# A perceiver layer on one core: the key tile between the two stages normalised by root and reciprocal, and the next projection put ahead of unit 0's transposes

## The chip, the core and the metric

The kernel runs on one core of a Trainium2 chip. A core has five engines with queues of their own, each of which works through its queue in order: PE (TensorE, matrix products and transposes), DVE (VectorE), ACT (ScalarE), POOL (GpSimd) and SP (which here only issues transfers). They wait for one another through semaphores. The metric is device time in microseconds (us), lower is better; of several runs the median is taken.

## What is computed

The layer is a cross-attention from 2 x 64 latent rows to 1024 context rows for each of two batches, then a self-attention and a gated feed-forward part. Only the first matters here:

```
k, v   = split((layernorm(ctx) ++ layernorm(latents)) @ Wkv)     # 1024 + 64 keys, 16 heads of 64
k      = k / max(norm(k per head) / 8, 1e-8) * kn_g
sim    = (q / max(norm(q per head) / 8, 1e-8) * qn_g / 8) @ k^T
attn   = softmax(sim, axis=-1)
out    = attn @ v, then @ Wout + bout, added to x
```

The two gain vectors go to the query side. The values are never formed: softmax(sim) is multiplied with the normalised context rows (`xn`), and the result with the value weights afterwards.

## The kernel before

**Items.** The rows of the context are cut into 16 tiles of 128, 8 for each batch, and one more tile holds the latents. With the queries that makes 18 items (`ITEMS`). For each item PE transposes the normalised rows (`norm_transposed`, 2 transposes into a PSUM bank), ACT and DVE split the result into a high and a low part (`xt_high` writes `xth`, `xt_low` writes `xtl`), and PE projects it on the keys (`project`, 12 matrix products of 512 columns, in `banks` 0 and 1 or 3 and 4). ACT squares the keys (`squares`), DVE sums the squares per head and clamps them (`key_norm2`, `key_clamp`), something takes the power -1/2 of the 128x16 sums, and DVE multiplies the keys by it out of PSUM (`key_scale`, two halves). PE transposes them (`keys_transposed`, 2 x 4), and ACT copies them out (`keys_out`).

**Stage one** is a loop over items 0 to 9 (`ITEMS_A` = 10), with the projection of item 10 behind it. Here the power is taken by a square root on ACT and a reciprocal on DVE.

**Stage two** is a loop over 16 units (`UNITS`; a unit is a pair of heads of one batch, 8 units for batch 0 and 8 for batch 1). In unit u PE transposes the exponentials (`probs_transposed`, parts 0, 1 and 2 with 4, 4 and 1 transposes), ACT and DVE split them (`probs_high` writes `pth`, `probs_low` writes `ptl`), PE computes the logits of unit u+1 (`logits`, parts 0, 1 and 2, with 3, 3 and 1 matrix products, in banks 3, 4 and 5) and then the mix of unit u (`mix`, 27 products). DVE takes the maximum with the mask (`logits_max`) and ACT the exponential (`exponentials`). From unit 1 on the logits of parts 0 and 1 use split operands: ACT writes `qh` and `kh` (`unit_high`), DVE `ql` and `kl` (`unit_low`), and only then can PE begin them. Units 0 to 7 carry one item each as well: unit u transposes the keys of item 10+u and projects item 11+u. For items from 10 on the power is taken by one POOL instruction (`ALU.pow`, line 451), and POOL's queue also holds the normalisation of the next context rows.

**The place between the stages.** PE transposes item 9's keys, computes unit 0's logits from unsplit operands, and then issues 12 matrix products on the identity matrix into bank 7 that compute nothing (`keep_clock(12, 7)`), while DVE and ACT make unit 0's exponentials. DVE works in the order `key_norm2(10)`, `key_clamp(10)`, `logits_max(0)`, `key_scale(10)`. ACT loads the table for the exponential, takes the exponentials, and goes into the unit loop, where its order for unit 0 is `probs_high(0, 0)`, `keys_out(10)`, `xt_high`, `unit_high(1)`, `probs_high(0, 1)`, `squares(11)`, `probs_high(0, 2)`.

The order is written out by hand in one function for each engine. Part 1 of unit 0's transposes goes to bank 7, parts 0 and 2 to bank 6. The profile counts a matrix product on fp32 data that are not split as two records, so `keep_clock(12, 7)` appears as 24.

Of the kernel before, what the change touches and what calls it, by code (L numbers as in the profile page):

```python
# [17 lines left out]
def perceiver_layer(nc, x, ctx, mask, ln_x_g, ln_x_b, ln_l_g, ln_l_b, qn_g, kn_g, Wq, Wkv, Wout, bout,  # L18
# [7 lines left out]
    G = H // 2  # L26
# [24 lines left out]
    with ExitStack() as stack:  # L51
# [257 lines left out]
        def t2_bank(i, h):  # L309
            return 2 if h == 0 else (6 if i < ITEMS_A else 0)  # L310

# [16 lines left out]
        def t3_bank(u, c):  # L328

            return 6 if c != 1 or 0 < u < G else (7 if u == 0 else 0)  # L330

# [71 lines left out]
        def _(pool):  # L403
# [44 lines left out]
            for i in range(ITEMS):  # L448
                if i >= ITEMS_A:
                    pool.wait_ge(n2_ready, i + 1)  # L450
                    nc.gpsimd.tensor_tensor(rn[:, i % 2, :], n2[:, i % 2, :], mhalf, ALU.pow).then_inc(rnp_ready, 1)  # L451
# [32 lines left out]
        def _(act):  # L484
# [141 lines left out]
            squares(ITEMS_A, 1)  # L626
            keys_out(ITEMS_A - 1, 0)
            keys_out(ITEMS_A - 1, 1)

            nc.scalar.activation(warm[:, 1:2], warm[:, 0:1], ACT.Exp)  # L630
            exponentials(0)
            context_high(ITEMS_A)
            for u in range(UNITS):
# [10 lines left out]
                if i < ITEMS:  # L644
                    keys_out(i, 0)
                    keys_out(i, 1)
                if i + 1 < ITEMS:
                    xt_high(tile(i + 1))
# [61 lines left out]
        def _(dve):  # L710
# [59 lines left out]
            def key_scale(i, h):  # L770
                if i >= ITEMS_A:
                    dve.wait_ge(rnp_ready, i - ITEMS_A + 1)
# [96 lines left out]
            key_clamp(ITEMS_A)  # L869
            logits_max(0)  # L870
            key_scale(ITEMS_A, 0)
            key_scale(ITEMS_A, 1)
            inverse_sum(0)
            for u in range(UNITS):
                i = ITEMS_A + u
                probs_low(u, 0)
                if i + 1 < ITEMS:
                    xt_low(tile(i + 1))
# [109 lines left out]
        def _(pe):  # L988
# [20 lines left out]
            def project(i, h):  # L1009

                if i >= ITEMS_A + 1:
# [28 lines left out]
            def keys_transposed(i, h):  # L1040
                pe.wait_ge(kn_ready, 2 * i + h + 1)
                if i > 0 and (h == 0 or i < ITEMS_A):
# [28 lines left out]
            def probs_transposed(u, c):  # L1071
                j0, j1 = T3[c]
                if c == 0:
                    pe.wait_ge(exp_ready, u + 1)
                if u == 0 or u > G:

                    if 3 * u + c - (1 if c == 2 else 2 if c == 1 else 0) > 0 and not (u == 0 and c == 1):
                        pe.wait_ge(ptl_ready, 3 * u + c - (1 if c == 2 else 2 if c == 1 else 0))
                elif u < G or c != 1:
                    pe.wait_ge(ptl_ready, 3 * u + c - (1 if u == G and c == 2 else 0))  # L1080
# [3 lines left out]
            def mix(u, parts=(0, 1, 2)):  # L1084
                b = u // G
                if u % G == 0:
                    pe.wait_ge(xnl_ready, NT * (b + 1))
                    pe.wait_ge(lns_ready, 1)
                if u == 0:
                    pe.wait_ge(ptl_ready, 2)  # L1090
                elif u >= G:
                    pe.wait_ge(o_ready, u - 1)
                else:
                    pe.wait_ge(o_ready, u)
# [59 lines left out]
            for u in range(UNITS - 1):  # L1154
                i = ITEMS_A + u
                probs_transposed(u, 0)
                if u >= G:
                    logits(u + 1, 0)
                if u > 0:
                    mix_transposed(u - 1)  # L1160
                if i < ITEMS:
                    keys_transposed(i, 0)
                    keys_transposed(i, 1)
                if i + 1 < ITEMS:
                    norm_transposed(tile(i + 1))
                probs_transposed(u, 1)
                if u >= G:
                    logits(u + 1, 1)
                if u > 0:
                    values(u - 1)  # L1170
                if i + 1 < ITEMS:
                    project(i + 1, 0)
                    project(i + 1, 1)
                if u < G:
                    logits(u + 1, 0)
                    logits(u + 1, 1)
                probs_transposed(u, 2)
                if w1T_first < u <= w1T_first + len(w1T_blocks):
# [139 lines left out]
```

## Time and profile before

| what | value |
|---|---|
| time, three runs | 246.96, 247.27, 247.66 us, median 247.27 |
| span of the profiled execution | 245.1 us |
| between that span and the median | 2.17 us |
| PE busy | 232.6 us (95%) |
| DVE busy | 154.8 us (63%) |
| ACT busy | 150.8 us (62%) |
| POOL busy | 79.6 us (32%) |

The profiled execution's own time is not listed, only its span from first to last instruction; what lies around it is taken as the difference to the median. Busy shares are averages over stages, so what a change at one place is worth must be read from the instructions at that place. In a row of a timeline the first number is the start and the second the time in which this group of instructions was busy; the bracket at the end tells how long the engine was idle before and what ended it.

### The profile page before, as it was taken

The page shows a single profiled execution, that of the slowest core. Times are in us where ns is not written, and L with a number is a line of the kernel's source. Part 1 is how long each engine was busy: PE and PEld are TensorE (multiplying, and loading weights), DVE is VectorE, ACT ScalarE, POOL GpSimd, SP SyncE. Part 2 cuts the span into 40 slices and gives each one's busy share as a digit, 9 for nine tenths or more (in the row PEclk, how much of TensorE's full clock was granted, in tenths as well). Part 3 has the DMA queues.
Part 4 walks back from the last instruction along what each step waited for, and adds up shares of the span by engine and source line. Part 5 has one row for each costly group of instructions (what it writes and reads, how often), then busy time and mean ns, then how long its engine had stood idle before and what let it go on. Part 6 is the DMA issues. An engine that isn't in the chain of part 4 may idle for free.

```text
span 245.1 us, 4234 instructions
## 1 busy us (share of the span) xinstructions
PE 232.6 (95%) x1509; PEld 199.7 (81%) x1509; DVE 154.8 (63%) x345; ACT 150.8 (62%) x328; POOL 79.6 (32%) x112
## 2 busy tenths in 40 slices
PE   6689999998999999999999999999999999999995
PEld 6464887876788888888888879999999888899884
DVE  1779999997687776867667655566664441303441
ACT  4354688877866768686756567777686754104141
POOL 5468776884453536464140600000000000100200
PEclk9799999999999999999999999999999999999999
DMA  5882111010000000000000899400000000000000
GB/s 180 306 276 95 47 28 38 21 45 0 21 3 0 0 4 1 0 3 0 0 3 0 261 417 322 121 3 0 0 4 0 3 1 0 3 0 0 3 0 21
DMA packets 11077, 13.67 MB, mean 56 GB/s; under 512 B 1553, under 2 KB 9777, under 8 KB 10801
## 3 DMA queue, kind: packets, MB, share of 16 engines
q1 hardware_dynamic: 10784, 12.88, 15.9%
q10 hardware_dynamic: 272, 0.52, 0.6%
q8 instruction: 12, 0.20, 0.3%
q14 instruction: 9, 0.07, 0.1%
HBM read 13.14 MB, written 0.13 MB: 54 GB/s over the span
## 4 chain that ended last, share of the span: by engine, by line
PE 74%; DVE 13%; DMA 3%; ACT 3%; issue 3%; POOL 2%; SPq 1%; ACTq 0%; POOLq 0%; DVEq 0%
PE banks L1103 23%; PE banks L991 13%; PE banks L1036 9%; PE banks L1065 8%; PE banks L1125 5%; PE banks L1222 4%; DVE small L761 4%; DMA rows<-in_L_xattn_ln_x_b 3%; PE banks L1118 3%; DVE sk L773 3%; PE banks L1067 3%; PE banks L1152 2%; DVE raw L729 2%; PE banks L1247 1%; DVE small L735 1%
## 5 line engine op out<-in xcount | busy, mean ns | idle before, releaser
L797 DVE TENSOR_TENSOR ptl<-banks,pth 128x512 fp32r<-128x512 f32 (+1 forms) x48 | 26.6, 555 | 32.6 <-ACT pth L562 32.0
L1103 PE MATMUL banks<-xnh,pth 128*128 128x256 f32 x128 | 37.5, 293 | 0.0
L1103 PE MATMUL banks<-xnl,pth 128*128 128x256 f32 x128 | 36.1, 282 | 0.0
L1103 PE MATMUL banks<-xnh,ptl 128*128 128x256 f32 x128 | 36.1, 282 | 0.0
L451 POOL TENSOR_TENSOR small<-small 128x16 f32<-128x16 f32 x8 | 23.3, 2907 | 35.4 <-DVE small L768 35.4
L562 ACT ACTIVATE pth<-banks 128x512 fp32r<-128x512 f32 (+1 forms) x48 | 23.6, 492 | 12.6 <-PE banks L991 10.9
L508 ACT ACTIVATE sk<-banks 128x512 f32<-128x512 f32 x36 | 20.6, 604 | 14.3 <-PE banks L1036 14.2
L413 POOL TENSOR_SCALAR tsm<-tsm 128x1 f32<-128x1 f32 x2 | 0.4, 190 | 88.8 <-DVE tsm L726 88.8
L773 DVE TENSOR_TENSOR sk<-banks,small 128x512 f32<-128x512 f32 x36 | 22.9, 678 | 7.2 <-POOL small L451 7.2
L761 DVE TENSOR_REDUCE small<-sk 128x8 f32<-128x512 f32 x36 | 23.5, 677 | 3.7 <-ACT sk L508 3.7
L1103 PEld LDWEIGHTS banks<-xnh,pth 128*128 128x128 f32 x128 | 24.4, 191 | 0.4 <-issue 0.4
L1103 PEld LDWEIGHTS banks<-xnl,pth 128*128 128x128 f32 x128 | 24.5, 191 | 0.0
L991 PE MATMUL banks<-ident,sp 128*128 128x128 f32 x144 | 24.3, 279 | 0.1
L1103 PEld LDWEIGHTS banks<-xnh,ptl 128*128 128x128 f32 x128 | 24.4, 191 | 0.0
L542 ACT ACTIVATE sp<-sp,small 128x1088 f32<-128x1088 f32 x16 | 19.3, 1205 | 8.3 <-DVE small L785 7.9
L1036 PE MATMUL banks<-wkh,xth 128*128 128x512 f32 x68 | 23.1, 421 | 1.0 <-ACT xth L491 1.0
L991 PE MATMUL banks<-ident,sk 128*128 128x128 f32 x152 | 21.5, 277 | 2.3 <-DVE sk L773 2.3
L1036 PE MATMUL banks<-wkh,xtl 128*128 128x512 f32 x68 | 21.7, 401 | 0.1
L1036 PE MATMUL banks<-wkl,xth 128*128 128x512 f32 x68 | 21.7, 401 | 0.0
L785 DVE CUSTOM_DVE_ANT_0 sp<-banks,mbias 128x1088 f32<-128x1088 f32 x16 | 20.4, 1275 | 1.4 <-PE banks L1067 1.2
L991 PEld LDWEIGHTS banks<-ident,sk 128*128 128x128 f32 x152 | 16.9, 140 | 5.3 <-DVE sk L773 4.3
L991 PEld LDWEIGHTS banks<-ident,sp 128*128 128x128 f32 x144 | 15.9, 137 | 3.2 <-DVE ptl L797 0.6
(176 smaller groups left out, 494.1 us busy)
## 6 DMA issues: line engine op xcount, KB each, us to landing
knT<-in_L_attn_qkv_kernel SPq DMA_DIRECT2D x1, 3072.0 KB, 13.7
raw<-in_ctx SPq DMA_DIRECT2D x16, 128.0 KB, 2.0
knT<-in_L_xattn_Wq SPq DMA_DIRECT2D x1, 1024.0 KB, 9.2
wv<-in_L_xattn_Wkv SPq DMA_DIRECT2D x1, 1024.0 KB, 5.2
wout_sb<-in_L_xattn_Wout SPq DMA_DIRECT2D x1, 1024.0 KB, 5.5
knT<-in_L_attn_out_kernel SPq DMA_DIRECT2D x1, 1024.0 KB, 16.3
wraw<-in_L_xattn_Wkv ACTq DMA_DIRECT2D x1, 512.0 KB, 4.1
wraw<-in_L_xattn_Wkv SPq DMA_DIRECT2D x1, 512.0 KB, 6.4
```

The source lines that it names most:

```text
L451: nc.gpsimd.tensor_tensor(rn[:, i % 2, :], n2[:, i % 2, :], mhalf, ALU.pow).then_inc(rnp_ready, 1)
L508: nc.scalar.activation(sk[:, i % 2, h * 512:(h + 1) * 512], banks[:, k_banks(i) + h, :], ACT.Square).then_inc(sq_ready, 1)
L542: nc.scalar.activation(sp2[:, u % 2, :], sp2[:, u % 2, :], ACT.Exp, bias=nmax[:, u:u + 1], scale=-1.0, accum_out=rsum[:, u:u + 1]).then_in ...
L562: nc.scalar.activation(pth[0:rows_, j0:j1, :], banks[0:rows_, t3_bank(u, c), 0:(j1 - j0) * P].rearrange("p (j r) -> p j r", j=j1 - j0), AC ...
L761: mark(nc.vector.tensor_reduce(n2[:, i % 2, 8 * h:8 * h + 8], sk[:, i % 2, h * 512:(h + 1) * 512].rearrange("p (h d) -> p h d", d=DH), AX. ...
L773: nc.vector.tensor_tensor(sk[:, i % 2, h * 512:(h + 1) * 512].rearrange("p (h d) -> p h d", d=DH), banks[:, k_banks(i) + h, :].rearrange(" ...
L785: nc.vector.tensor_tensor_reduce(out=sp2[:, u % 2, :], in0=logits_ps, in1=mbias[:, u // G, :], scale=-1.0, scalar=BIG, op0=ALU.add, op1=AL ...
L797: nc.vector.tensor_tensor(ptl[0:rows_, j0:j1, :], banks[0:rows_, t3_bank(u, c), 0:(j1 - j0) * P].rearrange("p (j r) -> p j r", j=j1 - j0), ...
L991: last = nc.tensor.transpose(dst[0:width, i * P:i * P + rows_], src(i), ident[0:rows_, 0:rows_])
L1036: last = nc.tensor.matmul(dst, a[:, n % 2, c, :], w[:, c, cols], start=(k == 0 and c == 0), stop=(k == 2 and c == DC - 1))
L1065: nc.tensor.matmul(dst, q_[:, u % 2, :], k_, start=(i == 0), stop=(i == 2))
L1103: last = nc.tensor.matmul(banks[:, u_bank(u), 0:D], p_[0:r, j, :], x_, start=(j == 0 and i == 0), stop=(j == NB - 1 and i == 2))
```

## The change

It touches only the passage from stage one to stage two and unit 0.

- Item 10's power is taken by a square root on ACT (between the two `keys_out` of item 9) and a reciprocal on DVE. POOL takes it from item 11 on.
- DVE runs `key_scale(10)` ahead of `logits_max(0)`.
- PE: `keep_clock(12, 7)` becomes `keep_clock(3, 7)`. Behind it stand the transposes of item 11's rows and of item 10's keys, then item 11's projection. Only then come unit 0's transposes, all three parts in a row, and the logits of unit 1.
- ACT runs `xt_high` of item 11 ahead of the exponentials, DVE runs `xt_low` of it behind `logits_max(0)`.
- Unit 0's transposes go to banks 3, 4 and 5, so each part of unit 1's logits now waits for the same part of `probs_low(0)`. Item 10's second key transposes go to bank 6 in place of bank 0.

```diff
         def t3_bank(u, c):
-            return 6 if c != 1 or 0 < u < G else (7 if u == 0 else 0)
+            if u == 0:
+                return 3 + c
+            return 6 if c != 1 or u < G else 0
...
             keys_out(ITEMS_A - 1, 0)
+            act.wait_ge(n2_ready, ITEMS_A + 1)
+            nc.scalar.activation(sd[:, ITEMS_A % 2, :], n2[:, ITEMS_A % 2, :], ACT.Sqrt).then_inc(sd_ready, 1)
             keys_out(ITEMS_A - 1, 1)
             nc.scalar.activation(warm[:, 1:2], warm[:, 0:1], ACT.Exp)
+            xt_high(tile(ITEMS_A + 1))
             exponentials(0)
             context_high(ITEMS_A)
...
             key_clamp(ITEMS_A)
-            logits_max(0)
+            dve.wait_ge(sd_ready, ITEMS_A + 1)
+            mark(nc.vector.reciprocal(rn[:, ITEMS_A % 2, :], sd[:, ITEMS_A % 2, :]))
+            dve.wait_ge(dchain, own[0])
             key_scale(ITEMS_A, 0)
             key_scale(ITEMS_A, 1)
+            logits_max(0)
+            xt_low(tile(ITEMS_A + 1))
             inverse_sum(0)
...
+                if u == 1:
+                    pe.wait_ge(ptl_ready, part + 1)
                 c0, c1 = ((0, 512), (512, 1024), (1024, KW))[part]
...
             for part in range(3):
                 logits(0, part)
-            keep_clock(12, 7)
+            keep_clock(3, 7)
+            norm_transposed(tile(ITEMS_A + 1))
+            keys_transposed(ITEMS_A, 0)
+            keys_transposed(ITEMS_A, 1)
...
             for u in range(UNITS - 1):
                 i = ITEMS_A + u
+                if u == 0:
+                    project(i + 1, 0)
+                    project(i + 1, 1)
+                    for c in range(3):
+                        probs_transposed(0, c)
+                    logits(1, 0)
+                    logits(1, 1)
+                else:
+                    probs_transposed(u, 0)
...
```

**PE, from unit 0's logits on.** `sp` is the exponentials of a unit, `sk` the keys of an item, `xn` the normalised rows, `ident` the identity matrix. Before:

```order
L1067 MATMUL banks<-knT,qbd 128x512 x2
L1067 MATMUL banks<-knT,qbd 128x64
L1125 MATMUL banks<-ident 128x128 x12
L991 MATMUL banks<-ident,sp 128x128 x4
L991 MATMUL banks<-ident,sk 128x128 x8
L991 MATMUL banks<-ident,xn 128x128 x2
L991 MATMUL banks<-ident,sp 128x128 x4
L1036 MATMUL banks<-wkh,xth 128x512 x2
```

and now:

```order
L1080 MATMUL banks<-knT,qbd 128x512 x2
L1080 MATMUL banks<-knT,qbd 128x64
L1136 MATMUL banks<-ident 128x128 x3
L1000 MATMUL banks<-ident,xn 128x128 x2
L1000 MATMUL banks<-ident,sk 128x128 x8
L1047 MATMUL banks<-wkh,xth 128x512 x2
L1047 MATMUL banks<-wkl,xth 128x512 x2
L1047 MATMUL banks<-wkh,xtl 128x512 x2
L1047 MATMUL banks<-wkh,xth 128x512 x2
L1047 MATMUL banks<-wkl,xth 128x512 x2
L1047 MATMUL banks<-wkh,xtl 128x512 x2
L1000 MATMUL banks<-ident,sp 128x128 x8
```

The first transposes of the exponentials stood ahead of the projection (L1036, L1047) and stand behind all of it now.

**ACT, over the same place.** L542 and L544 are the exponentials, L562 and L564 `probs_high`, L525 and L527 `keys_out`, L554 with L555 and L556 with L557 `unit_high`. Before:

```order
L630 ACT_TABLE_LOAD
L630 ACTIVATE warm<-warm 128x1
L542 ACTIVATE sp,small<-sp,small 128x1088 [waits max_ready]
L502 ACTIVATE xnh<-xn 128x256 [waits xn_ready]
L562 ACTIVATE pth<-banks 128x512 [waits u_ps,pt_ps]
L525 ACTIVATE knT<-banks 128x4x128 [waits lns_ready,kt_ps]
L525 ACTIVATE knT<-banks 128x4x128 [waits kt_ps]
L491 ACTIVATE xth<-banks 128x256 [waits k_ps,xt_ps]
L554 ACTIVATE qh<-qbd 128x128 [waits wk_lo,qbd_ready,kt_ready]
L555 ACTIVATE kh<-knT 128x1024
L562 ACTIVATE pth<-banks 128x512 [waits u_ps,pt_ps]
```

and now:

```order
L631 ACTIVATE small<-small 128x16 [waits n2_ready]
L527 ACTIVATE knT<-banks 128x4x128 [waits kt_ps]
L634 ACT_TABLE_LOAD
L634 ACTIVATE warm<-warm 128x1
L493 ACTIVATE xth<-banks 128x256 [waits k_ps,xt_ps]
L544 ACTIVATE sp,small<-sp,small 128x1088 [waits max_ready]
L504 ACTIVATE xnh<-xn 128x256 [waits xn_ready]
L564 ACTIVATE pth<-banks 128x512 [waits u_ps,pt_ps]
L527 ACTIVATE knT<-banks 128x4x128 [waits lns_ready,kt_ps]
L527 ACTIVATE knT<-banks 128x4x128 [waits kt_ps]
L556 ACTIVATE qh<-qbd 128x128 [waits wk_lo,qbd_ready,kt_ready]
L557 ACTIVATE kh<-knT 128x1024
```

`xth` moved ahead of the exponentials; `qh` and `kh` still stand behind the first `pth` and both copies of the keys.

**PE, from unit 1's logits to unit 0's mix.** L1065 and L1078 are products on the split operands, L1103 and L1114 the mix. Before:

```order
L1065 MATMUL banks<-kh,qh 128x512 [waits kh_ready,max_ready,kt_ready]
L1065 MATMUL banks<-kh,ql 128x512 [waits kl_ready]
L1065 MATMUL banks<-kl,qh 128x512
L1065 MATMUL banks<-kh,qh 128x512 [waits kh_ready]
L1065 MATMUL banks<-kh,ql 128x512
L1065 MATMUL banks<-kl,qh 128x512
L991 MATMUL banks<-ident,sp 64x128 [waits ptl_ready]
L1067 MATMUL banks<-knT,qbd 128x64
L1103 MATMUL banks<-xnh,pth 128x256 [waits ptl_ready,lns_ready,xnl_ready]
```

and now:

```order
L1000 MATMUL banks<-ident,sp 64x128
L1078 MATMUL banks<-kh,qh 128x512 [waits ptl_ready,kh_ready,max_ready,kt_ready]
L1078 MATMUL banks<-kh,ql 128x512 [waits kl_ready]
L1078 MATMUL banks<-kl,qh 128x512
L1078 MATMUL banks<-kh,qh 128x512 [waits kh_ready,ptl_ready]
L1078 MATMUL banks<-kh,ql 128x512
L1078 MATMUL banks<-kl,qh 128x512
L1080 MATMUL banks<-knT,qbd 128x64 [waits ptl_ready]
L1114 MATMUL banks<-xnh,pth 128x256 [waits ptl_ready,lns_ready,xnl_ready]
```

All three parts of the logits wait for `ptl` now, and the last of them, L1080, stands ahead of the mix.

## Rows read from the trace of the kernel before

**Rows 1.** The page: the chain of work that ended last, by engine.
```profile
PE 74%; DVE 13%; DMA 3%; ACT 3%; issue 3%; POOL 2%; SPq 1%; ACTq 0%; POOLq 0%; DVEq 0%
```

**Rows 2.** Busy time by stretch: start:end, length, then each engine, clock, DMA.
```profile
69.35:80.44 11.09, 11.09 (x75) 9.54 (x74) 8.86 (x19) 7.70 (x17) 5.78 (x6) 1.00 0.01 1
```

**Rows 3.** Timeline of PE between the stages: start, busy us, instructions, idle before.
```profile
57.48 2.05 PE L1067 MATMUL banks<-knT,qbd 128*128 128x512 f32 x6
59.37 2.90 PE L1125 MATMUL banks<-ident 128*128 128x128 f32 x24
62.25 0.66 PE L991 MATMUL banks<-ident,sp 128*128 128x128 f32 x4
62.75 1.04 PE L991 MATMUL banks<-ident,sk 128*128 128x128 f32 x8
...
64.94 0.70 PE L1036 MATMUL banks<-wkh,xth 128*128 128x512 f32 x2 [0.51 <-ACT xth L491]
...
67.77 0.39 PE L1065 MATMUL banks<-kh,qh 128*128 128x512 f32 x1
...
69.38 0.36 PE L1103 MATMUL banks<-xnh,pth 128*128 128x256 f32 x1
```

**Rows 4.** Timeline of DVE over the same place.
```profile
58.15 0.17 DVE L768 TENSOR_SCALAR small<-small 128x16 f32<-128x16 f32 x1
59.57 1.29 DVE L785 CUSTOM_DVE_ANT_0 sp<-banks,mbias 128x1088 f32<-128x1088 f32 x1 [1.24 <-PE banks L1067]
...
61.35 1.29 DVE L773 TENSOR_TENSOR sk<-banks,small 128x512 f32<-128x512 f32 x2 [0.49 <-POOL small L451]
...
65.97 0.66 DVE L806 TENSOR_TENSOR ql<-qbd,qh 128x128 fp32r<-128x128 f32 x1 [0.71 <-ACT kh L555]
66.55 1.21 DVE L807 TENSOR_TENSOR kl<-knT,kh 128x1024 fp32r<-128x1024 f32 x1
67.69 0.68 DVE L797 TENSOR_TENSOR ptl<-banks,pth 128x512 fp32r<-128x512 f32 x1
...
69.74 0.28 DVE L797 TENSOR_TENSOR ptl<-banks,pth 64x128 fp32r<-64x128 f32 x1
```

**Rows 5.** Timeline of POOL over the same place.
```profile
58.41 2.91 POOL L451 TENSOR_TENSOR small<-small 128x16 f32<-128x16 f32 x1 [3.25 <-DVE small L768]
...
65.74 0.74 POOL L431 TENSOR_TENSOR xnl<-xn,xnh 128x256 fp32r<-128x256 f32 x1
```

**Rows 6.** Timeline of one item of stage one: root (ACT) and reciprocal (DVE).
```profile
41.98 0.21 ACT L614 ACTIVATE small<-small 128x16 f32<-128x16 f32 x1 [0.28 <-DVE small L768]
...
42.62 0.24 DVE L854 RECIPROCAL small<-small 128x16 f32<-128x16 f32 x1
```

**Rows 7.** Timeline of ACT between the stages.
```profile
57.09 1.20 ACT L525 ACTIVATE knT<-banks 128x512 f32<-128x512 f32 x2 [0.34 <-PE banks L991]
58.30 1.28 ACT L630 ACT_TABLE_LOAD   x1
...
62.95 0.60 ACT L562 ACTIVATE pth<-banks 128x512 fp32r<-128x512 f32 x1 [0.44 <-PE banks L991]
63.44 1.08 ACT L525 ACTIVATE knT<-banks 128x512 f32<-128x512 f32 x2
64.39 0.41 ACT L491 ACTIVATE xth<-banks 128x256 fp32r<-128x256 f32 x1
64.66 0.33 ACT L554 ACTIVATE qh<-qbd 128x128 fp32r<-128x128 f32 x1
64.86 1.08 ACT L555 ACTIVATE kh<-knT 128x1024 fp32r<-128x1024 f32 x1
```

**Rows 8.** All instructions that write `ql`: durations in ns, least, median, greatest.
```profile
L806 DVE TENSOR_TENSOR ql<-qbd,qh x14: 277/280/759, 66.0 to 190.0; 128x128 fp32r<-128x128 f32 x14
```

**Rows 9.** Timeline of PE near the start of the kernel.
```profile
7.70 0.41 PE L991 MATMUL banks<-ident,knT 128*128 128x128 f32 x2 [1.85 <-DVE knT L824]
```

**Rows 10.** Busy time by stretch, as rows 2, for the stretch right behind it.
```profile
8.56:12.03 3.47, 3.35 (x7) 2.20 (x8) 2.75 (x5) 1.33 (x3) 2.20 (x4) 0.51 0.95 363
```

More of the change, by code:

```diff
@@ L309, in t2_bank @@
         def t2_bank(i, h):
-            return 2 if h == 0 else (6 if i < ITEMS_A else 0)
+            return 2 if h == 0 else (6 if i <= ITEMS_A else 0)
         w1T_first = G + 1
@@ L646, in _ @@
                     keys_out(i, 1)
-                if i + 1 < ITEMS:
+                if u > 0 and i + 1 < ITEMS:
                     xt_high(tile(i + 1))
@@ L770, in key_scale @@
             def key_scale(i, h):
-                if i >= ITEMS_A:
-                    dve.wait_ge(rnp_ready, i - ITEMS_A + 1)
+                if i > ITEMS_A:
+                    dve.wait_ge(rnp_ready, i - ITEMS_A)
                 nc.vector.tensor_tensor(
@@ L876, in _ @@
                 probs_low(u, 0)
-                if i + 1 < ITEMS:
+                if u > 0 and i + 1 < ITEMS:
                     xt_low(tile(i + 1))
@@ L1009, in project @@
             def project(i, h):
-                if i >= ITEMS_A + 1:
+                if i == ITEMS_A + 1:
+                    pe.wait_ge(kn_ready, 2 * i)
+                elif i > ITEMS_A + 1:
                     pe.wait_ge(kt_ready, 2 * i)
@@ L1041, in keys_transposed @@
                 pe.wait_ge(kn_ready, 2 * i + h + 1)
-                if i > 0 and (h == 0 or i < ITEMS_A):
+                if i > 0 and (h == 0 or i <= ITEMS_A):
                     pe.wait_ge(kt_ready, 2 * i - 1 + h)
@@ L1074, in probs_transposed @@
                     pe.wait_ge(exp_ready, u + 1)
[L1075 to L1079, printed above, removed]
+                if u == 1 and c == 0:
+                    pe.wait_ge(kt_ready, 2 * ITEMS_A + 2)
+                if u > G:
+                    pe.wait_ge(ptl_ready, 3 * u + c - (1 if c == 2 else 2 if c == 1 else 0))
+                elif 0 < u < G or u == G and c != 1:
                     pe.wait_ge(ptl_ready, 3 * u + c - (1 if u == G and c == 2 else 0))
@@ L1088, in mix @@
                     pe.wait_ge(lns_ready, 1)
-                if u == 0:
-                    pe.wait_ge(ptl_ready, 2)
-                elif u >= G:
+                if u >= G:
                     pe.wait_ge(o_ready, u - 1)
-                else:
+                elif u > 0:
                     pe.wait_ge(o_ready, u)
@@ L1155, in _ @@
                 i = ITEMS_A + u
[L1156 to L1171, printed above, removed]
+                if u == 0:
                     project(i + 1, 0)
                     project(i + 1, 1)
[L1174 to L1177, printed above, removed]
+                    for c in range(3):
[4 more added lines that the diff above has]
+                    probs_transposed(u, 0)
+                    if u >= G:
+                        logits(u + 1, 0)
+                    mix_transposed(u - 1)
+                    if i < ITEMS:
+                        keys_transposed(i, 0)
+                        keys_transposed(i, 1)
+                    if i + 1 < ITEMS:
+                        norm_transposed(tile(i + 1))
+                    probs_transposed(u, 1)
+                    if u >= G:
+                        logits(u + 1, 1)
+                    values(u - 1)
+                    if i + 1 < ITEMS:
+                        project(i + 1, 0)
+                        project(i + 1, 1)
+                    if u < G:
+                        logits(u + 1, 0)
+                        logits(u + 1, 1)
+                    probs_transposed(u, 2)
                 if w1T_first < u <= w1T_first + len(w1T_blocks):
```

2 lines of the change are left out of this document (1 added, 1 removed).

## The prediction

> **What bounds the kernel now.** I read the page's chain of waits first: three quarters of it is PE [rows 1]. Then the busy time of one unit of stage two: PE is busy in all of its 11.09 us at the full clock, while DVE, ACT and POOL have 2 us and more to spare [rows 2]. So in stage two time is PE's alone, and whatever delays PE at the head of the stage is not given back later; whatever PE gains there reaches the end in full. Then the timeline of PE between the stages [rows 3]. The logits of unit 0 start at 57.48, the filling products run from 59.37, and the next useful work, the first transposes of the exponentials, starts at 62.25. That hole is 2.88 us. A second one of 0.51 us stands ahead of item 11's projection at 64.94. Unit 1's logits start at 67.77 and unit 0's mix at 69.38. The mix is the point at which I compare: what stands behind it is as before in both kernels. At most 2.88 + 0.51 = 3.4 us can be won.
>
> The hole is not idle elsewhere: DVE waits for the logits, takes the maximum at 59.57 and then scales item 10's keys at 61.35 [rows 4], because the power on POOL runs from 58.41 to 61.32 [rows 5].
>
> **Part 1, item 10 by root and reciprocal.** DVE's clamp ends at 58.15 + 0.17 = 58.32 [rows 4]. A root takes 0.21 and a reciprocal 0.24 us [rows 6]. ACT is free, having finished the first half of the copies that start at 57.09 [rows 7], and has to hold back the second half, which nobody needs before the key transposes. With 0.05 for each hand-over DVE starts `key_scale(10)` at about 58.9, and its 1.29 us [rows 4] end at 60.2 instead of 62.64. `logits_max(0)` starts at 60.15 instead of 59.57. The exponentials follow it, so by the same distance that lies between the maximum (59.57) and PE's first transposes (62.25), 2.68 us, they would be ready for PE at 62.8. The table load (1.28 us, rows 7) moves by the root's wait to about 59.2 and is over at 60.7 with its warming instruction; `xt_high(11)` runs right behind it, and the maximum hides both.
>
> **Part 2, PE.** The three products that stay in the filler end at about 60.1. The transposes of the rows of item 11 wait for `key_scale(10)` at 60.2, so that is where useful work starts again: 2 + 8 transposes. In the filler 24 records take 2.90 us, 0.12 each [rows 3], so ten take 1.2 us, and the projection starts at 61.4 instead of 64.94: 3.5 us earlier. It lasts as before, from 64.94 to 67.77, 2.83 us, and ends at 64.2. Its low part `xtl` is made by 61.9 and is needed some 0.9 us after the projection's start, so it is hidden. Nine transposes of the exponentials take 1.1 us, and PE is ready for unit 1's logits at 65.3, ahead of the 67.77 of before. If nothing else were late, six products like those between 67.77 and 69.1 and the small one would put the mix at 66.9, 2.5 us early.
>
> **Part 3, what is late next.** It is not PE. The first transposes of the exponentials start at 64.2, where they started at 62.25, and ACT's queue for unit 0 hangs on them. Before, ACT took `pth` 0.70 us after their start (62.25 to 62.95), the keys' copies 0.49 later, and was through them at 64.39; `qh` needs 0.20 and `kh` 1.08 us [rows 7]. `xth` no longer stands between them, which saves 0.27. From PE's start at 64.2 this gives `pth` at 64.9, `qh` at 66.4, `kh` from 66.6 to 67.65, where it ended at 65.94 before. Behind `kh` comes DVE: `ql`, `kl`, `ptl` part 1, the sums of item 11, the clamp and `ptl` part 2, which ended at 70.02 before, 4.08 us after `kh` [rows 4]. In that row `ql` took 0.66 us, and it ended when POOL's `xnl` (65.74 to 66.48) had ended [rows 5]; the 14 rows of `ql` have a median of 0.28 [rows 8]. In the changed kernel POOL has no power to take for item 10 and does this step at 63.1, well before. I take 0.28: the chain is 3.70 us, `kl` is ready at 69.1 and `ptl` part 2 at 71.35. With the long `ql` it would be 0.38 later. The Trainium skill ("GPSIMD Engine Reference", Specifications) says the same of the two engines: GpSimd's SBUF interfaces are shared with VectorE, with contention when a DVE instruction has two SBUF inputs, as `ql` has. By that rule the cheap value holds here, since POOL is idle at 67.7.
>
> PE waits for all of it. The first product of unit 1's logits needs `kh` (67.65), the second `kl` (69.1), part 1 needs `ptl` part 1 (69.8), and the small part 2, which stands ahead of the mix and did not wait for this before, needs `ptl` part 2 (71.35). Two short records and the hand-over put the mix at 71.6 instead of 69.38: **2.2 us later**. The new waits on `ptl` are the price of the banks: before, PE used those of unit 1's logits at once, and now the exponentials' transposes lie in them.
>
> **Part 4, the clock.** Between 65.3 and 69.1 PE has one product of 0.23 us to do, and little until 71.4. At the start of the kernel PE was idle for 1.85 us, worked 0.41 us and was idle again [rows 9]; then the granted clock was 0.51 for 3.47 us, the lower level, 1.2 GHz, against 2.4 [rows 10]. The coming gap, about 2.3 us and then 1.3 us, is longer than that one, and the 12 filling products that bridged the old one are not there. So I expect the clock to fall here. What it costs depends on how much of a stretch of 3.47 us lies on the waits, where it is free, and how much on the mix: between 0 and half of it, 1.7 us. The gap begins 6.3 us before the mix, so part of the low stretch passes in it; I take 0.7 us, a little less than the middle. The Trainium skill ("TensorE: Matmul & The Clock Gate", Part 1) puts it the other way round, that the throttled state is the default and activity releases it, with half of the pulses passed and nothing in between; that speaks against taking filler away, and by it alone the mix would be slow until its own work has released the clock.
>
> **The sum.** Span 245.1 + 2.2 + 0.7 = 248.0. The median lies 2.17 us above this span, so 250.2 us.
>
> **Rivals.**
> A, late chain and a fallen clock, as summed: 250.2, between 249.5 and 251.2. For it: both orders are fixed in the code and the durations stand in rows.
> B, late chain, but the clock stays up or falls only in the waits: 247.27 + 2.2 = 249.5. For it: PE is never idle for longer than some 2.3 us at once.
> C, faster: the chain behind `pth` is ready in time and PE's early projection counts. Mix at 66.9, 247.27 - 2.5 = 244.8. It decides at one point: `kl` would have to be there by 65.5 and `ptl` part 2 by 66.7. Against it: `kh` stands behind `pth`, and `pth` behind the transposes, which now stand behind the projection.
> D, nothing comes of it: the delay is there, but unit 1 has slack and takes it up, or the chain shortens by 2 us, for instance with the projection done where DVE and ACT would else have waited for it. 247.3. Against it: PE is busy throughout a unit [rows 2].
> E, worse: the clock stays low for two such stretches, or falls again in unit 1: 2 x 1.7 on top of 2.2, about 252.9.
>
> **Chances.** A 0.52, B 0.24, C 0.09, D 0.07, E 0.08. Forecast 250.2 us. The range reaches from below B, with the hand-overs a few tenths shorter (248.9), to above A with the clock's full 1.7 and the long `ql` (251.6): it leaves out C, D, E and little of A. A change of 0.3% (0.74 us) is about what a measurement of this kernel can tell from none: faster than that 0.09, within it 0.07, slower 0.84.
>
> **What would show it.** Item 11's projection starting near 61.4 shows parts 1 and 2. `kh` starting near 66.6 and `kl` ending near 69.1, with PE idle in front of the second product of unit 1's logits, and again in front of the small product, shows part 3; the mix starting at 71.6 is its sum. A granted clock of 0.5 in a stretch of 67 to 75 shows part 4; if the clock stays at 1.0, B holds. I am wrong if `kh` starts before 65.5, or if the distance between the first mix products of units 0 and 1 is below 11.0 us, which would be slack that I say isn't there.

## The result, and the profile after

| | before | after |
|---|---|---|
| time | 247.12 us median of 4 runs (246.79 to 247.66) | 250.62 us median of 4 runs (250.50 to 251.42) |
| ratio | | 1.014 [1.012, 1.016] |
| span of the profiled execution | 245.1 us | 249.6 us |
| profiled execution's own time | not listed | 251.42 us |

The change makes the kernel 3.5 us slower; 250.2 was forecast. The profiled execution of after is the longest of its four: its span is 249.6 us, those of the other three are 248.7 to 248.8. It came 0.82 us later out of its startup than that of before: the logits of unit 0 start at 58.30 where they started at 57.48 [rows 3]. The other profiled kernels below start them at 57.99 to 58.97, with the same code up to there, so I compare distances from that start and not times.

The startup differs by how long PE is slow in it. A pair of products of the first projections in after:
```profile
15.60 1.05 PE L1047 MATMUL banks<-wkh,xth 128*128 128x512 f32 x2
```

The granted clock recorded over this place in after (busy time by stretch, columns as in [rows 2]):
```profile
14.00:17.00 3.00, 3.00 (x9) 2.32 (x9) 1.28 (x3) 1.29 (x3) 1.73 (x3) 1.00 0.51 134
```

The same view of experiment 1's kernel (below):
```profile
9.65:16.55 6.90, 6.52 (x16) 4.14 (x16) 4.33 (x9) 2.26 (x5) 4.95 (x9) 0.51 0.86 294
```

In experiment 1's kernel the clock is at the lower level for 6.9 us there, against 3.47 us in before [rows 10], and such a pair takes 1.05 us too (at 14.85). So the products of after run at the lower level until about 17.3, although its record says 1.00. Two things follow. The 0.82 us are probably a longer slow stretch at the start, which the change does not touch. And the mean clock of an execution can miss a slow stretch at the start, so below it is weak evidence; the lengths of PE's instructions are the better one.

The page of after, chain of waits by engine, which answers to [rows 1]: nearly the same, three quarters PE.
```profile
PE 75%; DVE 12%; DMA 3%; ACT 3%; issue 2%; POOL 2%; SPq 1%; ACTq 0%; POOLq 0%; DVEq 0%
```

Timeline of PE in after, between the stages (columns as in [rows 3]):
```profile
58.30 2.05 PE L1080 MATMUL banks<-knT,qbd 128*128 128x512 f32 x6
...
62.20 0.70 PE L1047 MATMUL banks<-wkh,xth 128*128 128x512 f32 x2
...
65.03 1.14 PE L1000 MATMUL banks<-ident,sp 128*128 128x128 f32 x9
68.52 0.47 PE L1078 MATMUL banks<-kh,qh 128*128 128x512 f32 x1 [2.35 <-ACT kh L557]
69.89 0.80 PE L1078 MATMUL banks<-kh,ql 128*128 128x512 f32 x1 [0.90 <-DVE kl L812]
70.48 0.63 PE L1078 MATMUL banks<-kl,qh 128*128 128x512 f32 x1
...
72.52 0.56 PE L1114 MATMUL banks<-xnh,pth 128*128 128x256 f32 x1
72.88 0.41 PE L1114 MATMUL banks<-xnl,pth 128*128 128x256 f32 x1
73.09 0.41 PE L1114 MATMUL banks<-xnh,ptl 128*128 128x256 f32 x1
...
75.82 0.28 PE L1114 MATMUL banks<-xnh,pth 128*128 128x256 f32 x1
...
77.31 0.28 PE L1114 MATMUL banks<-lnh,ptl 64*128 64x256 f32 x1
77.52 0.66 PE L1000 MATMUL banks<-ident,sp 128*128 128x128 f32 x4
...
88.39 0.28 PE L1114 MATMUL banks<-lnh,ptl 64*128 64x256 f32 x1
```

Two things are to be seen. First, PE does its work early: the projection starts at 62.20, only 3.90 us behind unit 0's logits, where it was 7.46 before. Then PE stands still twice, 2.35 us for `kh` and 0.90 for `kl`. Secondly, the products behind the second wait are about half as fast: a mix product starts 0.21 us behind the one ahead of it (72.88, 73.09), where it was 0.12 in before (69.58, 69.70). The rows' own lengths overlap, so they grow by less: `kl,qh` lasts 0.63 us and not 0.39, and a mix product 0.41 and not 0.28, until 75.8. From the start of the mix to the next unit's transposes it takes 77.52 - 72.52 = 5.00 us. In the other kernels below where the clock stayed up this takes 3.6, and in before 72.97 - 69.38 = 3.59.

The granted clock in after (busy time by stretch, columns as in [rows 2]):
```profile
67.00:68.00 1.00, 0.00 (x0) 0.00 (x0) 0.00 (x0) 1.00 (x3) 0.00 (x0) 1.00 0.00 0
68.00:69.00 1.00, 0.47 (x1) 0.19 (x1) 0.59 (x2) 1.00 (x3) 0.00 (x0) 0.96 0.00 0
69.00:70.00 1.00, 0.10 (x1) 0.11 (x1) 1.00 (x2) 1.00 (x4) 0.00 (x0) 0.50 0.00 0
...
75.00:76.00 1.00, 1.00 (x7) 1.00 (x7) 1.00 (x2) 0.43 (x2) 0.53 (x1) 0.63 0.00 0
```

PE does nothing from 67 to 68, when ACT is busy throughout with `kh` and what stands ahead of it. The clock falls to the lower level at about 69.0 and comes back at about 75.8. It stays low although PE works without a pause from 69.89 on.

ACT over the same place:
```profile
65.67 0.60 ACT L564 ACTIVATE pth<-banks 128x512 fp32r<-128x512 f32 x1 [1.81 <-PE banks L1000]
66.16 1.08 ACT L527 ACTIVATE knT<-banks 128x512 f32<-128x512 f32 x2
67.31 1.07 ACT L557 ACTIVATE kh<-knT 128x1024 fp32r<-128x1024 f32 x1
```

DVE over the same place:
```profile
59.72 1.29 DVE L778 TENSOR_TENSOR sk<-banks,small 128x512 f32<-128x512 f32 x2
...
68.41 0.29 DVE L811 TENSOR_TENSOR ql<-qbd,qh 128x128 fp32r<-128x128 f32 x1 [1.43 <-ACT kh L557]
68.62 1.22 DVE L812 TENSOR_TENSOR kl<-knT,kh 128x1024 fp32r<-128x1024 f32 x1
69.75 0.68 DVE L802 TENSOR_TENSOR ptl<-banks,pth 128x512 fp32r<-128x512 f32 x1
70.36 1.27 DVE L766 TENSOR_REDUCE small<-sk 128x8 f32<-128x512 f32 x2
...
71.74 0.28 DVE L802 TENSOR_TENSOR ptl<-banks,pth 64x128 fp32r<-64x128 f32 x1
```

ACT waits 1.81 us for the transposes that stand behind the projection (`pth`, 65.67), and only then come the keys' copies, `qh` and `kh`. DVE waits 1.43 us for `kh`. The last two `ptl` rows show the second half of the trouble: part 2, 64 rows high, waits behind item 11's sums and comes at 71.74. The chain that ended last runs through just these pieces (start, length, what):
```profile
67.44 0.95 ACT kh L557
...
68.70 1.15 DVE kl L812
...
69.89 2.50 PE banks L1078 x5
```

The difference of the spans is 4.5 us. It is 0.82 of startup, 14.22 - 11.90 = 2.32 from unit 0's logits to the mix (72.52 - 58.30 against 69.38 - 57.48), and 1.4 under the mix. Without the 0.82 it is 3.7, which is what the three other executions of after have over 245.1. From the mix's end on a unit lasts as before: the last product of the mix starts at 77.31 and again at 88.39, 11.08 us apart.

### The profile page after: what moved, and what is told of

The parts are those of the page before. It is cut to its first block, busy times and chain, and to the rows that moved or that the text cites. A ratio compares the mean times of both kernels' runs of the same rounds, so it can differ in the third digit from the quotient of the medians.

```text
span 249.6 us, 4201 instructions
## 1 busy us (share of the span) xinstructions
PE 235.9 (95%) x1491; PEld 201.9 (81%) x1491; DVE 154.2 (62%) x346; ACT 150.9 (60%) x329; POOL 77.0 (31%) x111
## 4 chain that ended last, share of the span: by engine, by line
PE 75%; DVE 12%; DMA 3%; ACT 3%; issue 2%; POOL 2%; SPq 1%; ACTq 0%; POOLq 0%; DVEq 0%
PE banks L1114 23%; PE banks L1000 14%; PE banks L1047 10%; PE banks L1078 8%; PE banks L1243 4%; PE banks L1136 4%; DVE small L766 3%; DMA rows<-in_L_xattn_ln_x_b 3%; DVE sk L778 3%; PE banks L1129 3%; PE banks L1080 3%; PE banks L1167 2%; DVE raw L734 2%; PE banks L1268 1%; PE banks L1301 1%
## 5 line engine op out<-in xcount | busy, mean ns | idle before, releaser
L1114 PE MATMUL banks<-xnh,pth 128*128 128x256 f32 x128 | 38.3, 299 | 0.0
L1114 PE MATMUL banks<-xnl,pth 128*128 128x256 f32 x128 | 36.8, 288 | 0.0
L1114 PE MATMUL banks<-xnh,ptl 128*128 128x256 f32 x128 | 36.7, 287 | 0.0
L564 ACT ACTIVATE pth<-banks 128x512 fp32r<-128x512 f32 (+1 forms) x48 | 23.6, 492 | 13.1 <-PE banks L1000 11.4
L453 POOL TENSOR_TENSOR small<-small 128x16 f32<-128x16 f32 x7 | 20.4, 2909 | 35.9 <-DVE small L773 35.9
L1114 PEld LDWEIGHTS banks<-xnh,pth 128*128 128x128 f32 x128 | 25.2, 197 | 0.4 <-issue 0.4
L544 ACT ACTIVATE sp<-sp,small 128x1088 f32<-128x1088 f32 x16 | 19.3, 1205 | 10.0 <-DVE small L790 9.6
L1114 PEld LDWEIGHTS banks<-xnl,pth 128*128 128x128 f32 x128 | 25.2, 197 | 0.0
L1114 PEld LDWEIGHTS banks<-xnh,ptl 128*128 128x128 f32 x128 | 25.1, 196 | 0.0
L1047 PE MATMUL banks<-wkh,xth 128*128 128x512 f32 x68 | 23.8, 432 | 0.5 <-ACT xth L493 0.5
L1047 PE MATMUL banks<-wkl,xth 128*128 128x512 f32 x68 | 22.6, 415 | 0.0
L1047 PE MATMUL banks<-wkh,xtl 128*128 128x512 f32 x68 | 22.3, 411 | 0.0
```

What stands on the lines that cost most here:

```text
L544: nc.scalar.activation(sp2[:, u % 2, :], sp2[:, u % 2, :], ACT.Exp, bias=nmax[:, u:u + 1], scale=-1.0, accum_out=rsum[:, u:u + 1]).then_in ...
L564: nc.scalar.activation(pth[0:rows_, j0:j1, :], banks[0:rows_, t3_bank(u, c), 0:(j1 - j0) * P].rearrange("p (j r) -> p j r", j=j1 - j0), AC ...
L1047: last = nc.tensor.matmul(dst, a[:, n % 2, c, :], w[:, c, cols], start=(k == 0 and c == 0), stop=(k == 2 and c == DC - 1))
L1114: last = nc.tensor.matmul(banks[:, u_bank(u), 0:D], p_[0:r, j, :], x_, start=(j == 0 and i == 0), stop=(j == NB - 1 and i == 2))
```

## The experiments

Eight kernels were run, each with the kernel before measured beside it; experiments 4, 6, 7 and 8 ran on another chip than the rest. "Distance" is always the time from the start of unit 0's logits to the start of its mix in the profiled execution: 11.90 us before, 14.22 after. The theory: `kh` and `kl` hang behind the first `pth` in ACT's queue, and that behind the projection, 2.2 us; the small `ptl` hangs behind item 11's sums; the fallen clock comes on top, as a consequence of the wait. The rival for the chain: the new bank waits or PE's order itself cost the time, and the order on ACT and DVE is harmless.

**1. `kh` ahead of the exponentials.** After, with unit 1's splits taken out of the queue behind `pth`:

```diff
             xt_high(tile(ITEMS_A + 1))
+            unit_high(1)
             exponentials(0)
...
-                if u == 0:
-                    unit_high(1)
                 probs_high(u, 1)
...
             xt_low(tile(ITEMS_A + 1))
+            unit_low(1)
             inverse_sum(0)
...
-                if u == 0:
-                    unit_low(1)
                 probs_low(u, 1)
```

> The changed kernel with one thing moved: ACT makes unit 1's qh and kh before unit 0's exponentials, and DVE makes ql and kl right behind xtl of item 11. Nothing else moves. My theory (PE waits for kh and kl, which stand behind the first pth and the copies of item 10's keys): kl is ready before PE has done unit 0's transposes, the first products of unit 1's logits start about 67.0 (changed kernel's own time, where it was 68.5), the last wait is for ptl part 2, which still stands behind the sums of item 11, and the mix starts near 70.4 instead of 72.5. That is 2.1 us, and PE's longest gap becomes about 1.1 us, so the clock can stay up (1.4 us more): 247.1 us, or 248.5 if the clock still falls. Rival (the new waits of the logits on ptl, which come with banks 3 to 5, are the whole cause): kh and kl are not what PE waits for, 250.6 as the changed kernel.

Measured: 247.76 us (247.02 to 248.0, 10 runs), the kernel before, beside it, 247.47 (19 runs), ratio 1.0014 [1.0003, 1.0026]. Distance 70.40 - 58.37 = 12.03. PE:
```profile
67.31 0.47 PE L1076 MATMUL banks<-kh,qh 128*128 128x512 f32 x1 [1.07 <-ACT knT L527]
...
68.58 0.50 PE L1076 MATMUL banks<-kh,qh 128*128 128x512 f32 x1 [0.33 <-DVE ptl L801]
...
70.16 0.43 PE L1078 MATMUL banks<-knT,qbd 128*128 128x64 f32 x2 [0.62 <-DVE ptl L801]
70.40 0.36 PE L1112 MATMUL banks<-xnh,pth 128*128 128x256 f32 x1
```

One move of two steps gives back nearly all of the 3.5 us: 2.19 at the mix, and the clock stays at 1.00. PE's order and the bank waits are untouched, so neither is enough to make the kernel 3.5 us slower. It is 0.7 above the 247.1 expected, of which 0.35 is that the kernel before, too, was slower beside it. The rows say what is late next: 0.33 and 0.62 us for `ptl`, parts 1 and 2, and 1.07 us ahead of the first product. The row names the keys' copies (`knT`) for that one, but in experiment 3's kernel the same product waits as long and does not wait for them to end:
```profile
66.50 1.08 ACT L527 ACTIVATE knT<-banks 128x512 f32<-128x512 f32 x2
...
66.94 0.47 PE L1083 MATMUL banks<-kh,qh 128*128 128x512 f32 x1 [1.07 <-DVE ptl L805]
```

So it is `ptl` part 0: the new wait that came with the banks, 1.07 us. In after it is hidden, since `kh` comes later still.

**2. The wait filled with products.** After, with 14 products on the identity between unit 0's transposes and unit 1's logits, so that PE is busy in the wait and nothing is faster:

```diff
                     for c in range(3):
                         probs_transposed(0, c)
+                    keep_clock(14, 7)
                     logits(1, 0)
```

> The changed kernel with 14 filling products (28 records, 3.2 us) put between unit 0's transposes and unit 1's logits, where PE was idle for 2.35 and 0.90 us. They compute nothing. Theory (the clock falls because of this gap, and the low clock under the mix costs 1.4 us and some 0.2 under the logits): the clock stays at 1.0 from 66 to 77, the second product of the logits still starts near 69.9, when kl is ready, and the time is 249.0 us. Rival (the clock falls because 9 of the 12 filling products ahead of it were taken away, wherever the gap is): still a stretch at 0.5, 250.6. Second rival (filler only delays the logits): above 250.6.

Measured: 249.62 us (249.16 to 249.99, 4 runs), ratio 1.0089 [1.007, 1.0107]. PE:
```profile
66.10 3.29 PE L1136 MATMUL banks<-ident 128*128 128x128 f32 x28
...
69.98 0.51 PE L1078 MATMUL banks<-kh,ql 128*128 128x512 f32 x1 [0.35 <-DVE kl L812]
...
72.16 0.43 PE L1080 MATMUL banks<-knT,qbd 128*128 128x64 f32 x2 [0.60 <-DVE ptl L802]
72.40 0.37 PE L1114 MATMUL banks<-xnh,pth 128*128 128x256 f32 x1
```

The stretch of the wait and the mix, columns as in [rows 2]:
```profile
66.00:76.00 10.00, 9.04 (x67) 7.66 (x64) 7.34 (x15) 6.80 (x14) 3.62 (x2) 1.00 0.01 2
```

The clock does not fall, and the delay is there: distance 72.40 - 58.38 = 14.02, 2.12 more than before. This parts the two terms. The chain alone costs 0.89%, 2.2 us, with an interval of 1.7 to 2.6. The clock is the rest of after's 1.4%: 0.5% or 1.3 us by the ratios, whose intervals lie apart but close (at most 1.0107, at least 1.012), so that its size rests on the trace; by the profiled executions 1.6, of which 0.2 lies ahead of the mix (14.22 - 14.02) and 1.4 under it (5.00 us against 3.60).

**3. And the splits of the exponentials ahead of item 11's work.** Experiment 1, and ACT takes `pth` parts 1 and 2 ahead of the keys' copies and the squares, DVE `ptl` part 2 ahead of item 11's sums (the same rows are taken out at their old places for unit 0):

```diff
+                if u == 0:
+                    probs_high(0, 1)
+                    probs_high(0, 2)
                 if i < ITEMS:
                     keys_out(i, 0)
                     keys_out(i, 1)
...
                 probs_low(u, 1)
+                if u == 0:
+                    probs_low(0, 2)
...
-                probs_low(u, 2)
+                if u > 0:
+                    probs_low(u, 2)
```

> As the run with kh early, and also: ACT makes pth parts 1 and 2 of unit 0 ahead of the copies of item 10's keys and of item 11's squares, and DVE makes ptl parts 1 and 2 ahead of item 11's sums. Theory (the delay is all in the order of ACT and DVE, and PE's early projection is worth its 2.5 us once nothing stands behind it): logits of unit 1 from 67.0 to 68.4, mix at 68.6 where the changed kernel has 72.5, clock stays up, 245.3 us, 1.8 us faster than the kernel before. Rival (the delayed copies of item 10's keys and squares of item 11 come back as a wait in unit 1): mix early, but the distance from unit 0's mix to unit 1's above 11.1 us, 246 to 247.

Measured: 246.44 us (246.31 to 246.58, 4 runs), ratio 0.9961 [0.9946, 0.9976]. Distance 68.55 - 57.99 = 10.56, 1.34 less than before. But the next mix follows 80.15 - 68.55 = 11.60 us later, not 11.09 as in [rows 2]. PE, the first products of the two mixes:
```profile
68.55 0.36 PE L1119 MATMUL banks<-xnh,pth 128*128 128x256 f32 x1
...
80.15 0.36 PE L1119 MATMUL banks<-xnh,pth 128*128 128x256 f32 x1
```

The chain of waits of the same kernel between them (start, length, what):
```profile
68.09 1.29 DVE small L769 x2
...
69.66 2.92 POOL small L453
...
72.60 0.70 DVE sk L781
```

PE is fast now, and the work that was pushed back is late in its turn: the squares of item 11 come behind the keys' copies, the sums and POOL's 2.92 us behind them, and the keys of item 11 are scaled at 72.60 when PE wants to transpose them. That is the rival that its expectation named, and it explains 0.5 of the 1.1 us that the run lies above 245.3. The rest is small: 0.35 us are those by which the kernel before, beside it, lies above 247.12, and 0.26 are at the mix. It was expected at 68.6 in after's own time, which is a distance of 10.30, and 10.56 came; that it starts at 68.55 is only the earlier startup.

**4. The squares ahead of the keys' copies.** This tests that reading: experiment 3 with ACT's squares of item 11 in front of `keys_out(10)`.

```diff
                     probs_high(0, 2)
+                    squares(i + 1, 0)
+                    squares(i + 1, 1)
                 if i < ITEMS:
                     keys_out(i, 0)
```

> As the run with kh and the splits early, and also ACT squares item 11 ahead of the copies of item 10's keys. In that run unit 1 had 11.6 us from mix to mix in place of 11.1, and its chain went over the copies, the squares, the sums, the power on POOL and the scaling of item 11. Theory (unit 1 waits for item 11's power because it starts late, 0.5 us): the squares start 1 us earlier, so does POOL, the distance from mix to mix is back at 11.1 and the time is 245.9 us. Rival (the copies, now later, hold unit 1's first transposes through bank 6): distance still 11.6 or more, 246.4 or above.

Measured: 246.53 us (246.11 to 246.94, 5 runs), the kernel before, beside it, 247.8 (17 runs), ratio 0.9943 [0.9931, 0.9956]. Distance 68.63 - 58.06 = 10.57, and the next mix 79.72 - 68.63 = 11.09 us behind it:
```profile
68.63 0.36 PE L1121 MATMUL banks<-xnh,pth 128*128 128x256 f32 x1
...
79.72 0.36 PE L1121 MATMUL banks<-xnh,pth 128*128 128x256 f32 x1
```

The half microsecond at unit 1 is gone in the trace. By the ratios the gain over experiment 3 is 0.2% with intervals that overlap, so it stands on the trace. The median itself lies where its rival had it (246.4 or above), but experiments 3 and 4 were measured on different chips, whose kernels before differ by 0.3 us; ratios, not times, are to be compared.

**5. Before, with the short filler.** Only `keep_clock(12, 7)` made `keep_clock(3, 7)`, to ask whether the gap of the kernel before alone brings the clock down.

```diff
-            keep_clock(12, 7)
+            keep_clock(3, 7)
```

> The kernel before with 3 filling products in place of 12 between the stages, so that PE is idle from about 60.1 to 62.25. No useful work is touched. Theory (the clock falls in gaps of this length when nothing fills them): a stretch at 0.5 that begins near 62 and lies under useful work for up to 3.5 us, 247.1 plus up to 1.7, about 248.3. Rival (a gap of 2.15 us alone does not bring the clock down): 247.1, no change; then the clock of the changed kernel fell only because of its second gap.

Measured: 247.56 us (246.78 to 248.76, 10 runs), ratio 1.0014 [0.9996, 1.0033]. In the profiled execution PE was idle for 2.00 us. PE's row behind the gap:
```profile
62.91 0.66 PE L991 MATMUL banks<-ident,sp 128*128 128x128 f32 x4 [2.00 <-ACT sp L542]
```

The clock stayed up in the ten microseconds that follow (busy time by stretch):
```profile
63.00:73.00 10.00, 9.50 (x63) 8.39 (x63) 7.45 (x16) 7.64 (x15) 4.66 (x5) 1.00 0.06 15
```

Neither expectation held for all runs. Seven lie between 246.78 and 247.71 with mean clocks of 0.986 to 1.0, as the kernel before does (19 runs beside it, 246.87 to 247.74 us, 0.984 to 1.0). The three others took 248.36, 248.43 and 248.76 us, each at a mean clock of 0.979. They may be executions in which the gap brought the clock down, about 1.0 us dearer, while it left it alone in others. That is not shown: none of the three is the profiled one. A slower startup is a rival, since the startups of the profiled kernels differ by up to 1.5 us, and experiment 7's kernel, which has its filler, has a run at a mean clock of 0.979 too (248.86 us) that does not stand out from its other eight.

**6. The first transposes between the halves of the projection.** After, and PE makes the first four transposes of unit 0 halfway through. This pulls the head of the ACT chain forward and leaves ACT's order alone.

```diff
                     project(i + 1, 0)
+                    probs_transposed(0, 0)
                     project(i + 1, 1)
-                    for c in range(3):
-                        probs_transposed(0, c)
+                    probs_transposed(0, 1)
+                    probs_transposed(0, 2)
```

> The changed kernel with one thing moved: PE does the first four transposes of unit 0's exponentials between the two halves of item 11's projection instead of behind both. ACT's and DVE's orders stay. Theory (ACT's queue hangs on these transposes, and everything up to the mix follows at a fixed distance): they start 1.4 us earlier, kh, kl and ptl too, and the mix starts 1.4 us earlier, 249.2 us; if PE's gaps are then too short for the clock to fall, another 1.4, 247.8. Rival (PE is simply filled and the delay lies in the waits on ptl alone): 250.6.

Measured: 249.61 us (248.28 to 251.22, 7 runs), ratio 1.0071 [1.0046, 1.0096]. Distance 71.83 - 58.97 = 12.86. PE:
```profile
64.33 0.60 PE L1000 MATMUL banks<-ident,sp 128*128 128x128 f32 x4
...
67.83 0.47 PE L1078 MATMUL banks<-kh,qh 128*128 128x512 f32 x1 [0.96 <-ACT kh L557]
69.20 0.70 PE L1078 MATMUL banks<-kh,ql 128*128 128x512 f32 x1 [0.90 <-DVE kl L812]
...
71.83 0.56 PE L1114 MATMUL banks<-xnh,pth 128*128 128x256 f32 x1
```

The transposes come 65.03 - 58.30 - (64.33 - 58.97) = 1.37 us earlier than in after, and the mix 14.22 - 12.86 = 1.36 us earlier: everything behind them moved by what they moved, one for one. That is the head of the chain, shown from PE's side, as experiment 1 showed its middle. The clock fell here too in the profiled execution, with waits of 0.96 and 0.90 us only; the products from 69.69 on are 0.63 us long, and those of the mix are back at 0.28 from 72.9 on. But the spread of the seven runs is 2.9 us, with mean clocks from 0.970 (249.83 us) to 0.991 (248.28, but also 249.69), so its median says little of the chain, and the distance has to carry it. The kernel before, beside it, had 247.8.

**7. The root alone.** Before, with item 10's power by root and reciprocal and its scaling ahead of the maximum; PE's order is untouched.

```diff
+            act.wait_ge(n2_ready, ITEMS_A + 1)
+            nc.scalar.activation(sd[:, ITEMS_A % 2, :], n2[:, ITEMS_A % 2, :], ACT.Sqrt).then_inc(sd_ready, 1)
             keys_out(ITEMS_A - 1, 1)
...
-            logits_max(0)
+            dve.wait_ge(sd_ready, ITEMS_A + 1)
+            mark(nc.vector.reciprocal(rn[:, ITEMS_A % 2, :], sd[:, ITEMS_A % 2, :]))
+            dve.wait_ge(dchain, own[0])
             key_scale(ITEMS_A, 0)
             key_scale(ITEMS_A, 1)
+            logits_max(0)
```

> The kernel before with only the first part of the change: item 10's power by root and reciprocal, and DVE scales its keys ahead of unit 0's maximum. PE's order and all fillers stay. Theory (the part by itself buys nothing, since PE's next work in the old order is the transposes of the exponentials, and it delays the maximum by some 0.6 us): PE's first transposes 0.6 us later, 247.9 us. Rival (POOL's 2.9 us for the power bounded the gap): faster than 247.2.

Measured: 248.6 us (247.98 to 249.02, 9 runs), the kernel before, beside it, 247.8, ratio 1.0023 [1.0011, 1.0035], which is 0.6 us. Distance 71.17 - 58.77 = 12.40, 0.5 more than before:
```profile
64.06 0.66 PE L996 MATMUL banks<-ident,sp 128*128 128x128 f32 x4 [0.51 <-ACT sp L542]
...
71.17 0.36 PE L1108 MATMUL banks<-xnh,pth 128*128 128x256 f32 x1
```

The exponentials' transposes start 5.29 us behind unit 0's logits and not 4.77, because the maximum stands behind the scaling. By itself this part of the change is a small loss. It pays only through what it lets PE do early, the key transposes and the projection.

**8. The best order found.** Experiment 4, with the exponentials back ahead of `kh`, and experiment 6's transposes.

```diff
             xt_high(tile(ITEMS_A + 1))
-            unit_high(1)
             exponentials(0)
+            unit_high(1)
...
                     project(i + 1, 0)
+                    probs_transposed(0, 0)
                     project(i + 1, 1)
```

> As the run with the squares first, with two further moves: ACT takes unit 0's exponentials ahead of kh, and PE does the first four transposes between the halves of item 11's projection. Theory (what is left in front of unit 1's logits is the wait for ptl part 0, 1.07 us, which stands behind the transposes): ptl part 0 is then made behind kl and not 1.4 but only some 0.35 us earlier, 245.5 us. Rival (kh now waits behind the exponentials and becomes the late one again): same as or slower than the run with the squares first, 245.9 or more.

Measured: 246.12 us (245.81 to 246.52, 5 runs), ratio 0.993 [0.9916, 0.9943]. Distance 68.54 - 58.19 = 10.35. It is 1.7 us faster than the kernel before and the fastest of all. Against experiment 4 the ratio is 0.13% lower, with overlapping intervals, so the ratios do not show a gain; the trace has 0.22 us, where 0.35 were expected. PE:
```profile
66.95 0.47 PE L1085 MATMUL banks<-kh,qh 128*128 128x512 f32 x1 [0.87 <-DVE ptl L807]
```

So rival C's mechanism, PE's early projection, is real: once the queues of ACT and DVE follow PE's new order, 1.55 of the 2.5 us that PE alone would allow arrive at the mix. Most of what is missing is the wait of 0.87 us in the row above, for `ptl` part 0, which the change itself brought in with the banks.

## Why the prediction was right

The forecast was 250.2 us (248.9 to 251.6), slower with a chance of 0.84; measured were 250.62. Point by point, with the profiled times of after less the 0.82 us of startup:

| step | forecast | after, less 0.82 |
|---|---|---|
| scaling of item 10's keys starts | 58.9 | 58.90 |
| projection of item 11 starts | 61.4 | 61.38 |
| first transposes of the exponentials | 64.2 | 64.21 |
| `pth` | 64.9 | 64.85 |
| `kh` starts | 66.6 | 66.49 |
| `kl` ready, PE's second product | 69.1 | 69.07 |
| mix starts | 71.6 | 71.70 |
| low clock under the mix | 0.7 us | 1.4 us |

- **Parts 1 and 2** held to 0.02 us. The projection did start 3.5 us earlier, counted from the same startup, and none of it reached the end.
- **Part 3, the chain.** It held to 0.1 us: every duration in it came from a row of the kernel before, and only the starting point moved. The choice of the short `ql` was right, 0.29 us [rows 8], at 68.41 with POOL idle until 71.91. In experiment 7 POOL splits its rows at the same time as `ql` is made, and `ql` took 0.66 again. The Trainium skill ("GPSIMD Engine Reference", Specifications) has the two engines share SBUF interfaces, and both figures agree with it. Experiments 1 and 6 show that this chain is the cause. One detail is off: I had PE wait for the last `ptl` just ahead of the mix. In after no wait of PE for `ptl` shows, since the half-speed products ran until 72.19 and `ptl` part 2 was there at 72.02. In experiment 2, where they are fast, the wait is there (0.60 us), and the mix starts at 14.02 behind unit 0's logits, where the forecast has 71.6 - 57.48 = 14.1. That the mix's row of the table agrees to 0.1 in after itself is luck: there the low clock and not `ptl` set the start of the mix.
- **Part 4, the clock, is the term that was mis-sized.** That it would fall was right, and in experiment 2, with the wait filled, it stayed up. I took 0.7 us, from one stretch of 3.47 us part of which would pass in the waits. It began at 69.0, when most of the waiting was over, and it was 6.8 us long, two such stretches. Some 0.9 us of it passed in the wait for `kl`. The 2.6 us under the logits cost only 0.2, since the mix would have had to wait for `ptl` anyway, as it does in experiment 2. The 3.3 us under the mix cost 1.4. The weak step was to take the length from one row: the same place at the start of the kernel, which gave me 3.47 us, shows 6.9 in experiment 1's kernel. My rival E had the two stretches, but at 2 x 1.7 us, since it took both in full; the measured sum lies between A and E, and nearer to A.
- **The sum.** By the profiled spans: 245.1 + 0.82 + 2.32 + 1.41 = 249.65, against 249.6 measured. By the medians: 3.5 us, of which 2.2 is the chain (experiment 2) and 1.3 the clock; the forecast had 2.2 + 0.7. The time around the span, which I took as 2.17 us, is 251.42 - 249.6 = 1.82 in the profiled execution of after. The trace of before was thus probably an execution some 0.3 us shorter than the median: two runs of that kernel beside experiment 1 with spans of 245.1 took 246.87 and 246.89.
- **The rivals.** B was refuted by the windows: the clock fell and cost time. D needed slack in unit 1, and the unit lasted as before. C was refuted for this kernel and turned out to be one order of ACT and DVE away.

What stays open: how the clock decides. The gaps of after (2.35 and 0.90 us) and of experiment 6 (0.96 and 0.90) brought it down in the executions that were profiled; those of experiment 5 (2.00) and experiment 1 (1.07, 0.33, 0.62) did not. How often each does so in the other executions isn't known. Also open is whether the early projection pays without the root: that combination was not run.

## What to carry to other kernels

When one engine's work is put in a new order, write down for each of the other engines what its queue holds ahead of the thing that the first engine now wants next. The step that moved (here the exponentials' transposes) drags everything behind its reader along, needed or not. The repair is often to move two instructions in those queues, and then to look for what those pushed back, as the squares of item 11 here. Filler that looks like waste may be what keeps the clock up: count its removal as a cost wherever the new order leaves a gap.

## What the hardware showed that I had not expected

- The clock stayed at the lower level for 6.8 us, at least 5.9 of them with PE at work throughout (69.89 to 75.8). At the start of the kernel the low stretch was 3.47 us in before [rows 10] and 6.9 in experiment 1.
- The granted clock can be recorded as 1.00 while products take as long as at the lower level (after, 14 to 17 us: 1.05 us for a pair of products, as in experiment 1's kernel at 0.51).
- Of ten executions with a gap of 2.00 us (experiment 5) three were about 1.0 us longer; the profiled one kept its clock. If the gap is the reason, which isn't shown, a single profile can show the harmless case.
- Waits of 0.96 and 0.90 us with one product between them came ahead of a fallen clock in experiment 6. I had thought only of gaps above 2 us.
